# The end of a block-quantised FFN kernel: last tile whole, late residuals on GpSimd, bias and residual matmuls moved ahead

## The reference

```python
def _L0_cond_ref(x, conditions, weights):
    w = weights[conditions]
    return jnp.einsum('bct,bcd->bdt', x, w)
...
        amax = jnp.max(jnp.abs(xb), axis=-1, keepdims=True)
        exp = jnp.floor(jnp.log2(jnp.maximum(amax, jnp.finfo(x.dtype).tiny))) - FP4_EMAX
        scale = jnp.where(amax > 0, jnp.exp2(exp), jnp.ones_like(amax))
        q = jnp.clip(xb / scale, -FP4_MAX, FP4_MAX)
        aq = jnp.abs(q)
        lsb = jnp.where(aq < 2.0, 0.5, jnp.where(aq < 4.0, 1.0, 2.0))
        qr = jnp.round(q / lsb) * lsb
...
    a = _quant_dequant_mxfp4(input.reshape(-1, orig_shape[-1]))
    w = _quant_dequant_mxfp4(weight)
    out = jnp.einsum('mk,nk->mn', a, w) + bias
...
x = x + _L0_ffn_ref(_L0_cond_ref(x, itok_B_1_198, L0_cond_weights), L0_ffn_weight, L0_ffn_bias)
```

## Time and profile before

| What | Value |
|---|---|
| Time, median of 3 runs | 96.83 us (96.57 to 97.84) |
| The profiled execution's own time | 95.26 us |
| Its span in the trace | 93.6 us |
| Busy: TensorE, VectorE, ScalarE, GpSimd | 81.6, 83.2, 74.5, 30.2 us |
| Granted TensorE clock, mean | 0.992 |

### The profile page before, as it was taken

One profiled execution on the slowest core, in us unless ns is written; L12 is line 12 of the kernel. 1 busy time (PEld: TensorE's weight loads), 2 busy tenths in 40 slices (PEclk: granted clock), 3 DMA queues, 4 the chain that ended last, 5 costly groups with the idle time before them and its releaser, 6 DMA issues.

```text
span 93.6 us, 2117 instructions
## 1 busy us (share of the span) xinstructions
PE 81.6 (87%) x695; PEld 40.7 (44%) x695; DVE 83.2 (89%) x149; ACT 74.5 (80%) x86; POOL 30.2 (32%) x57
## 2 busy tenths in 40 slices
PE   4998596996899998999899989989989999999600
PEld 4995273592483334332433423343334344335300
DVE  1188989999999999999999999999999999999900
ACT  3736099998997949999999999999999997956000
POOL 4478776997787003002100500040012003030000
PEclk9999999999999999999999999999999999999996
DMA  1988598999999999999999995589179859939894
GB/s 30 334 301 277 124 374 263 352 329 285 333 282 300 347 294 326 194 251 240 270 270 294 329 257 107 224 220 214 42 248 244 159 221 239 210 80 281 318 313 138
DMA packets 14683, 23.20 MB, mean 248 GB/s; under 512 B 4178, under 2 KB 4946, under 8 KB 14674
## 3 DMA queue, kind: packets, MB, share of 16 engines
q1 hardware_dynamic: 11744, 17.83, 63.2%
q0 software_dynamic: 2256, 4.21, 21.3%
q10 hardware_dynamic: 674, 1.05, 3.6%
HBM read 11.54 MB, written 8.39 MB: 213 GB/s over the span
## 4 chain that ended last, share of the span: by engine, by line
PE 46%; ACT 11%; DVE 8%; issue 6%; DVEq 0%; ACTq 0%
PE o_ps L378 24%; PE y_ps L331 6%; ACT o_sb L528 5%; PE o_ps L373 4%; ACT y_sb L507 4%; PE y_ps L378 4%; PE o_ps L359 2%; PE o_ps L343 2%; DVE last_x L809 2%; DVE top L694 2%; DVE a L703 1%; DVE x_sb L804 1%; PE y_ps L359 1%; PE o_ps L405 1%; PE y_ps L343 1%
## 5 line engine op out<-in xcount | busy, mean ns | idle before, releaser
L378 PE MATMUL o_ps<-wT,aT 128*128 128x512 bf16 x104 | 24.9, 380 | 0.0
L331 PE MATMUL y_ps<-x_sb,mix 64*64 64x512 f32 x128 | 16.8, 609 | 4.7 <-ACT y_sb L507 3.2
L675 DVE TENSOR_TENSOR n_int<-y_sb,inv 128x1024 int16<-128x1024 f32 (+1 forms) x18 | 19.6, 1099 | 0.3
L307 POOL DMA_DIRECT2D x_sb<-o_sb x6 | 6.1, 1014 | 41.7 <-ACT o_sb L528 41.7
L499 ACT ACTIVATE z<-y_ps 128x1024 bf16<-128x1024 bf16 x16 | 16.2, 1036 | 3.8 <-PE y_ps L331 3.6
L203 POOL DMA_DIRECT2D mix<-in_L_cond_weights_dram x32 | 16.7, 522 | 5.5 <-issue 4.2
L405 PE MATMUL o_ps<-idle 128*128 128x128 bf16 x202 | 15.3, 243 | 1.2 <-DVE idle L708 1.2
L507 ACT COPY y_sb<-y_ps 128x1024 f32<-128x1024 f32 x16 | 16.3, 1037 | 0.0
L405 PEld LDWEIGHTS o_ps<-idle 128*128 128x128 bf16 x202 | 13.8, 110 | 2.8 <-issue 2.5
L378 PEld LDWEIGHTS o_ps<-wT,aT 128*128 128x128 bf16 x104 | 9.1, 98 | 12.0 <-issue 2.7
L515 ACT ACTIVATE zone<-inv 128x1024 int16<-128x1024 int16 (+1 forms) x13 | 12.0, 941 | 0.3 <-DVE inv L668 0.3
(11 more groups left out here) (59 smaller groups left out, 76.4 us busy)
## 6 DMA issues: line engine op xcount, KB each, us to landing
x_sb<-in_x_dram SPq DMA_DIRECT2D x7, 1024.0 KB, 10.8
out_dram<-x_sb SPq DMA_DIRECT2D x16, 256.0 KB, 3.4
x_sb<-o_sb POOLq DMA_DIRECT2D x6, 512.0 KB, 5.6
out_dram<-x_sb SPq DMA_DIRECT2D x5, 512.0 KB, 2.8
w_sb<-in_L_ffn_weight_dram SPq DMA_DIRECT2D x4, 256.0 KB, 3.7
last_x<-in_x_dram SPq DMA_DIRECT2D x4, 256.0 KB, 8.2
x_sb<-in_x_dram SPq DMA_DIRECT2D x1, 512.0 KB, 6.0
mix<-in_L_cond_weights_dram SPq DMA_DIRECT2D x32, 16.0 KB, 7.5
```

What stands on the lines that cost most here:

```text
L331: last = nc.tensor.matmul(y_ps[HALVES[g], 2 * q + r, :], mix[HALVES[r], (step - 1) * GROUP + n, :], x_tiles(step, n)[HALVES[r], :], start= ...
L378: last = nc.tensor.matmul(o_bank(step, t), aT[:, t, c, :], wT[:, c, :], start=False, stop=(c == KC - 1))
L675: nc.vector.tensor_tensor(columns(n_int, t, n), columns(y_sb[:, step % 2, :, :], t, n), columns(inv, t, n), ALU.mult).then_inc(n_done, 1)
```

## The change

Seven things change:

- Step 8's tile 3 is multiplied, biased and added whole, and stored by two DMAs (one per queue) where there were four.
- Step 7's tiles 2 and 3: ScalarE copies their PSUM to a new buffer `late_sb` (`copy_later`, between the second and third `copy_turned_last`). GpSimd adds x in one 128 x 1024 operation and stores both tiles by one DMA. The two VectorE adds and SyncE's two stores of them go.
- In the loop over steps, the bias matmuls of pair 0 stand before `mix_pair(step + 3, 0)` instead of after it.
- For step 7, `residual_pair` and the bias of pair 0 stand before the first `turn_pair`, and both `turn_pair` stand together.
- ScalarE's four `zone_pair` of step 8 now stand together before `copy_late`; before, the fourth stood after the first `copy_turned_last`.
- `round_w` for weights 0 and 1 is split in two, the first half standing before `tree_1` of weights 2 and 3. `round_w` for 2 and 3 is one operation before `tree_1(1)`.
- `tree_3(4)` of the pipeline's start now follows the `rescale` of weights 2 and 3.

```diff
@@ sync
-            for t in range(SUMMED, GROUP):
-                sp.wait_ge(added, t - SUMMED + 1)
-                store(LAST - 1, t)
-            for t in range(GROUP - 1):
-                sp.wait_ge(added, t + 3)
-                store_last(sp, t, 0, slice(0, N), stored)
-            for half in range(2):
-                sp.wait_ge(added, GROUP + 2 + half)
-                store_last(sp, GROUP - 1, 0, n_half(half), stored)
+            for t in range(GROUP):
+                sp.wait_ge(added, t + 1)
+                store_last(sp, t, 0, stored)
@@ gpsimd
+            pool.wait_ge(late_copied, 4)
+            late_x = x_tiles(LAST - 1, SUMMED, 2)
+            nc.gpsimd.tensor_tensor(late_x, late_sb[:, :, :].rearrange("p t n -> p (t n)"), late_x, ALU.add
+                                    ).then_inc(late_added, 1)
+            pool.wait_ge(late_added, 1)
+            n0 = (LAST - 2) * GROUP + SUMMED
+            pool.dma_start(out_dram[:, n0:n0 + 2, :], late_x.rearrange("p (n t) -> p n t", n=2)
+                           ).then_inc(late_stored, 16)
@@ tensor, the loop over steps
-                    for q in range(2):
-                        ffn_pair(step - 1, q)
+                    ffn_pair(step - 1, 0)
+
+                    pe.wait_ge(aT_ready, tiles_done(step - 1, 3))
+                    bias_pair(step - 1, 1)
+                    ffn_pair(step - 1, 1)
...
+                bias_pair(step, 0)
                 if step + 3 <= LAST:
                     mix_pair(step + 3, 0)
@@ tensor, step 7 and the end
+            pe.wait_ge(y_copied, tiles_done(LAST, 1))
+            residual_pair(LAST - 1, 0)
+            bias_pair(LAST - 1, 0)
             pe.wait_ge(y_copied, tiles_done(LAST, 3))
             pe.wait_ge(a2_done, late_part(0))
             turn_pair(LAST - 1, 0, straight=True)
-            residual_pair(LAST - 1, 0)
-            for t in range(2):
-                bias_tile(LAST - 1, t, start=False)
             pe.wait_ge(a2_done, late_part(1))
             turn_pair(LAST - 1, 1)
...
-            bias_half(0)
-
-            pe.wait_ge(aT_ready, tiles_done(LAST, 2))
-            bias_half(1)
-            ffn_tile(LAST, 2)
-            for half in range(2):
-                ffn_half(half)
+            bias_tile(LAST, 3)
+            for t in range(2, GROUP):
+                ffn_tile(LAST, t)
@@ scalar
+            def copy_later():
+                act.wait_ge(o_ready, tiles_done(LAST - 1, GROUP - 1))
+                nc.scalar.copy(late_sb[:, :, :], y_ps[:, SUMMED:GROUP, :]).then_inc(late_copied, 2)
...
-            for t in range(GROUP - 1):
+            for t in range(GROUP):
                 zone_pair(after(LAST), late_part(1), t, 1)
             copy_late()
-            copy_turned_last(0)
-            zone_pair(after(LAST), late_part(1), GROUP - 1, 1)
-            for t in range(1, GROUP):
+            for t in range(GROUP):
                 copy_turned_last(t)
+                if t == 1:
+                    copy_later()
@@ vector
             invert(1, 0, 2)
+            round_w(0, 1)
             tree_1(0, 2, 2, z_count=GROUP)
-            round_w(0, 2)
+            round_w(1, 1)
...
-            round_w(2, 1)
+            round_w(2, 2)
             tree_1(1)
-            round_w(3, 1)
...
-            for t in range(SUMMED, GROUP):
-                dve.wait_ge(o_ready, tiles_done(LAST - 1, t))
-                nc.vector.tensor_tensor(x_tiles(LAST - 1, t), o_bank(LAST - 1, t), x_tiles(LAST - 1, t), ALU.add
-                                        ).then_inc(added, 1)
```

More of the change, by code:

```diff
@@ L162, in late_part @@
             return after(LAST - 1) + part
-        def n_half(half):
-            return bass.ds(half * (N // 2), N // 2)
         def t_pair(step, q):
@@ L181, in o_bank @@
                 return y_ps[:, t, :]
[L182 to L186 removed]
+            return (o_ps[:, 0, :], o_ps[:, 3, :], y_ps[:, 0, :], y_ps[:, 1, :])[t]
         block = ctx.enter_context(nc.Block())
@@ L204, in load_mixes, with store_last @@
                                 table[bass.ds(row, 1), :, :].rearrange("o c d -> (o c) d")).then_inc(mix_in[step], 16)
-        def store_last(queue, t, g, part, done):
-            queue.dma_start(exchanged_dram[LAST - 1, t // 2, g, t % 2, :, part], last_x[HALVES[g], t, part]
+        def store_last(queue, t, g, done):
+            queue.dma_start(exchanged_dram[LAST - 1, t // 2, g, t % 2, :, :], last_x[HALVES[g], t, :]
                             ).then_inc(done, 16)
@@ L380, in ffn_tile, with bias_pair, ffn_pair @@
                 last.then_inc(o_ready, 1)
-            def bias_half(half):
-                row = half * 32
-                nc.tensor.matmul(last_half(half), ones[row:row + 3, :], bias3[row:row + 3, n_half(half)],
-                                 start=True, stop=False)
-            def ffn_half(half):
-                pe.wait_ge(aT_ready, tiles_done(LAST, GROUP - 1))
-                for c in range(KC):
-                    last = nc.tensor.matmul(last_half(half), aT[:, GROUP - 1, c, :], wT[:, c, n_half(half)],
-                                            start=False, stop=(c == KC - 1))
-                last.then_inc(o_ready, 1)
-            def ffn_pair(step, q):
-                pe.wait_ge(aT_ready, tiles_done(step, 2 * q + 1))
+            def bias_pair(step, q):
                 for t in (2 * q, 2 * q + 1):
                     bias_tile(step, t, start=(q == 1))
+            def ffn_pair(step, q):
                 for t in (2 * q, 2 * q + 1):
@@ L442, in _ @@
                     residual_pair(step, 0)
+                if step == 1:
+                    pe.wait_ge(ones_ready, 1)
+                    pe.wait_ge(bias3_in, 16 * 2 * 3)
+                bias_pair(step, 0)
                 if step + 3 <= LAST:
                     mix_pair(step + 3, 0)
-            for q in range(2):
-                ffn_pair(LAST - 2, q)
+            ffn_pair(LAST - 2, 0)
+            pe.wait_ge(aT_ready, tiles_done(LAST - 2, 3))
+            bias_pair(LAST - 2, 1)
+            ffn_pair(LAST - 2, 1)
+            pe.wait_ge(y_copied, tiles_done(LAST, 1))
+            residual_pair(LAST - 1, 0)
+            bias_pair(LAST - 1, 0)
             pe.wait_ge(y_copied, tiles_done(LAST, 3))
@@ L596, in _ @@
             copy_turned(LAST - 1, 1)
-            for t in range(GROUP - 1):
+            for t in range(GROUP):
                 zone_pair(after(LAST), late_part(1), t, 1)
             copy_late()
-            copy_turned_last(0)
-            zone_pair(after(LAST), late_part(1), GROUP - 1, 1)
-            for t in range(1, GROUP):
+            for t in range(GROUP):
                 copy_turned_last(t)
-            for t in range(GROUP - 1):
-                act.wait_ge(added, t + 3)
-                store_last(act, t, 1, slice(0, N), others_stored)
-            for half in range(2):
-                act.wait_ge(added, GROUP + 2 + half)
-                store_last(act, GROUP - 1, 1, n_half(half), others_stored)
+                if t == 1:
+                    copy_later()
+            for t in range(GROUP):
+                act.wait_ge(added, t + 1)
+                store_last(act, t, 1, others_stored)
         @block.vector
@@ L800, in _ @@
             rescale(LAST, late_part(1 + GROUP), 2 * LAST + 1 + GROUP, GROUP - 1, 1)
-            for t in range(SUMMED, GROUP):
-                dve.wait_ge(o_ready, tiles_done(LAST - 1, t))
-                nc.vector.tensor_tensor(x_tiles(LAST - 1, t), o_bank(LAST - 1, t), x_tiles(LAST - 1, t), ALU.add
-                                        ).then_inc(added, 1)
             dve.wait_ge(last_x_in, 16 * GROUP)
-            for t in range(GROUP - 1):
+            for t in range(GROUP):
                 dve.wait_ge(o_ready, tiles_done(LAST, t))
                 nc.vector.tensor_tensor(last_x[:, t, :], o_bank(LAST, t), last_x[:, t, :], ALU.add).then_inc(added, 1)
-            for half in range(2):
-                dve.wait_ge(o_ready, tiles_done(LAST, GROUP - 1) + half)
-                part = last_x[:, GROUP - 1, n_half(half)]
-                nc.vector.tensor_tensor(part, last_half(half), part, ALU.add).then_inc(added, 1)
 _INS = ["x", "itok_B_1_198", "L0_cond_weights", "L0_ffn_weight", "L0_ffn_bias"]
```

30 lines of the change are left out of this document (11 added, 19 removed).

## The result

The changed kernel took 97.69 us (median of 6 runs, 96.54 to 98.77) beside 96.70 us for the kernel before (6 runs, 95.12 to 98.61). It is 1.019, with a 95% interval of 1.0135 to 1.0246: about two per cent slower. The forecast was 96.5 us and a small gain. The profiled execution took 97.26 us with a span of 95.4 us and a mean granted clock of 0.978. The lower clock is not the cause: in both traces it is 1.00 up to 87.95, where TensorE's last matmul of the changed kernel ends, and falls only behind that.

What follows compares the result with a forecast made beforehand. VectorE's stream bounds the middle; a DMA store backlog, as much as the last add, sets the end. Backlog (93.25) and GpSimd's chain (93.35) tie, so the span falls 93.6 to 93.3: 96.83 - 0.3 = 96.5 us, range 95.7 to 97.9.

Steps and rivals of the forecast that it cites:

- the part on GpSimd's add: End of kernel: add 2.3 us, store issued 87.05, landing 92.95, end 93.35, a tie with the DMA traffic's 93.25.
- The ring: Loop over steps, ScalarE and TensorE taking turns: bias hidden in a wait, one turn 8.64 to 8.32 us.
- Step 7: Residual and bias before the transposes: weight matmuls start at 78.03 instead of 78.39, 0.36 us gained.
- The add of GpSimd: Step 7's late residuals: one add taking 2.3 us, between 1.28 and 3.8, breaking even at 2.55.
- VectorE: Step 8: its last add ends at 88.4 instead of 88.89, 0.5 us earlier.
- SyncE's last issue: Final stores: four issues instead of seven, the last starting at 88.45 instead of 90.53.
- GpSimd's store of step 6: Late in the kernel: issued 1.05 us earlier, at 81.8 instead of 82.84.
- The backlog: Final stores on the DMA engines: 83.4 + 8.5 + 0.45 of holes ends traffic at 92.35, 0.35 us earlier.
- GpSimd is the end: Rival, chance 0.27: GpSimd's add and its store set the end, later than before from 2.55 us on; 97.4 us.
- Issues, not bytes: Rival, chance 0.18: holes between the final stores vanish, end at 91.75 at best, 0.95 us earlier; time 95.9.
- Nothing in the loop: Rival, chance 0.10: bias not hidden, loop turn stays 8.64 us, step 7 loses 0.1, traffic ends 93.0; 97.1 us.
- The chance of 0.07 for slower by two per cent: Whole kernel: slower by over 1.94 us was given 0.07, needing a GpSimd add of over 4.5 us.

## Why the prediction was wrong

The measured 97.69 us lies inside the stated range of 95.7 to 97.9. That is the width of the range and no success: the forecast was a gain of 0.3, and by the ratio the kernel lost about 1.8 us.

**The failed step** is in the part on GpSimd's add: the store "lands 5.9 later, at 92.95; the span's last 0.4 behind it makes 93.35. This is a tie". The 0.4 came from the hardware queues, 93.19 to 93.6. Behind a landing of GpSimd's own DMA stand 1.93 to 1.98 us of its closing instruction and 0.23 more, 2.2 in all. With 2.2 in place of 0.4 the same sum says 95.15; the span ended at 95.4. The nearness is in part luck: the store was issued 0.66 later than forecast (87.71 for 87.05) and took 0.43 less to land (5.47 for 5.9). The row that could have told it was in the kernel before: landed 88.69, closed 90.63. That is below what the views of the profile list, but the earlier trace rows had the landing, and no row there priced what follows a GpSimd landing. I used another queue's price where I should have given it bounds.

**The ring** of TensorE and ScalarE was priced rightly: 8.32 forecast, 8.32 measured, and step 6's copy out came 1.08 earlier (76.20 to 75.12) where I had taken 1.05. What I said the profile would show, copies out 8.4 apart and transposes within 0.2 of `a`, holds only from step 6 on: before it TensorE is still catching up. **Step 7** came out at 78.06 for 78.03, and this is luck in part: `a` was ready 0.31 earlier than before where I took 0.15, and the weight matmuls followed the second transposes by 0.65 where I took 0.46. The step 8 matmuls (83.4, 83.44) hang on it. `copy_late` came 0.2 later (from 81.14 to 81.35) for a forecast of 0.4. **The add of GpSimd** took 2.37 for 2.3, a value chosen between 1.28 and 3.8. It falls just short of the 2.55 at which I said that the add breaks even; the true break-even with the closing in it is 1.8 us lower, 0.75, far under the 2.34 that the fastest of these adds took. The Trainium skill's figure (GPSIMD Engine Reference, "Elementwise — side-by-side cycle accounting") had given an estimated 2.25 for the add, and the trace agrees to 0.12 us.

**VectorE** ended at 88.66, forecast 88.4. **SyncE's last issue** started at 88.69, forecast 88.45.

**GpSimd's store of step 6** failed in sign: forecast 1.05 earlier (81.8), measured 1.4 later (84.26). The issue of the accumulating DMA before it did come 1.08 earlier, but I took its landing time as fixed, and it grew from 5.0 to 7.5 us, with SyncE's stores issued beside it. It held the add up by about 0.25 us (`copy_later` was done at 84.79, the add started at 85.04). Of the loss it is a small part.

**The backlog** was forecast to end at 92.35 and ended at 93.83. This is the second step that failed. I took its work as the 8.5 us of before. From 82.00 on the engines were busy for 9.8 us (0.85 x 1.25 + 0.83 x 10.58), and in it they moved 3.0 MB (215 x 1.25 + 261 x 10.58) where it was 2.6 (279 x 9.45), which is the same rate. The bytes of the whole run are the same (23.20 MB), but 0.4 MB that had moved by 82.00 before was still to come, with the last accumulating DMA landing at 83.97 and not at 82.55. The holes were 2.0 us from 82.00 on, where I had 0.45 from 83.4 on. The traffic alone would have put the end at about 94.6, without GpSimd's closing, so 0.8 of the 1.8 us in the profile is the closing and 1.0 the traffic. The runs give the closing more than this one profile: 1.5% between GpSimd's and SyncE's store on the kernel before (1.017 and 1.002) and 1.6% on the changed one (1.019 and 1.003), of about 96 us. The share of the traffic is not settled: the loop alone measured 0.999, and the traffic ends between 92.8 and 94.7 in profiles of kernels with the new loop, and between 92.7 and 94.9 in those with the old one.

**Of the rivals,** "GpSimd is the end" (0.27) named the right engine and a time of 97.4 near the measured 97.69. Its mechanism was a slow add, and the add was not slow. What I had against it, that a store which starts by 90.7 finds the traffic still running, was true of the landing (93.18 against 94.16) and beside the point. "Issues, not bytes" was wrong: SyncE issued its last at 88.69 for 90.53 and nothing came earlier; the whole tile alone measured 1.005. "Nothing in the loop" was wrong as to the loop's ring. The chance of 0.07 for slower by two per cent was too low: the rival's chance lacked the term that every GpSimd store at the end pays. The measured 1.019 stands at that bound.

## What to carry to other kernels

Ask of the last work on each queue not when it lands but when its engine has closed: on GpSimd, a DMA of its own had to land some 1.8 us before the last one of SyncE's or ScalarE's here, or the span grew. If an idle engine takes over late work, let SyncE issue the store of it (1.017 with GpSimd's queue here, 1.002 with SyncE's). When a step brings a transfer forward, look at what is in flight at its new time before you move its landing by the same amount.

## What the runs showed of the hardware

- GpSimd's closing instruction ends 1.93 to 1.98 us after the landing of its own last DMA, at 2 KB (1.97) as at 512 KB (1.93 to 1.98), or 3.85 us after the end of an add that is its last work, whichever is later. SyncE is through 0.2 to 0.3 us after the last landing. ScalarE's closing ended before its own last store had landed, in every trace.
- A 512 KB accumulating DMA of GpSimd, from the third of a kernel on, landed in 5.0 to 5.9 us when it started 0.8 and 1.4 us behind SyncE's two stores (the order of before), and in 7.1 to 8.1 in the changed kernel, where a store of SyncE started within 0.25 us of it. At 0.54 us behind the second store it took 5.3 to 6.4 in three traces, and 6.4 and 7.4 in a fourth.
- GpSimd added 128 x 1024 elements of four bytes, both inputs in SBUF, in 2.34 to 2.37 us; VectorE took 1.28 for the same number with one input in PSUM, by the row of two in the earlier trace rows.
